# Four image layers on one core: another order of full layers and causal pieces, merged score matmuls, and work moved from VectorE to ScalarE and GpSimd

## The chip, the core and the metric

The kernel runs on one core of one Trainium2 chip. The metric is the device time of one execution in microseconds (us), lower is better; the time before is the median of three runs. The engines are TensorE (PE; its weight loads are PEld), VectorE (DVE), ScalarE (ACT), GpSimd (POOL) and SyncE (SP), which issues the DMAs.

## The reference, cut to what matters

x is float32, (4, 256, 32, 32): four batches of 256 channels and 1024 pixels. Four layers follow each other, each batch for itself:

- **L0**: attention over the 1024 pixels with 32-wide queries and keys, `gamma * out + x`.
- **L1** and **L3**: group normalisation (32 groups), attention over the 1024 pixels with 256-wide queries, keys and values, an output projection, and the residual.
- **L2**: the pixels as 1024 tokens of 256 values. Token normalisation, causal attention with 8 heads of 32 that share one key and value head, an output projection added to the tokens, token normalisation with gain and shift, then a feed-forward part: normalisation, a 256x256 product, normalisation, gelu, a 256x256 product, and the residual.

```python
x = _L0_conv_ref(x, ...)
x = _L1_conv_ref(x, ...)
x = _L2_conv_ref(x, ...)
x = _L3_conv_ref(x, ...)
```

## The kernel before, in words

There are two chains of work, woven on every engine. The **full chain** (F) holds the twelve full layers L0, L1 and L3 of the four batches in the order `FULL` (line 35). The **causal chain** (C) holds a few weight products and then L2 of batches 0 to 3, in the order that `causal_schedule` (line 159) gives. Each chain is a generator that yields after every step. `ORDER` (line 43) has a string for each engine, one letter a step: on PE, `F` or a digit takes the next full step, `C` or a letter a to h the next causal one, and the digit or the letter a to h also names the PSUM bank at which the step opens its unit. Every engine works through its string in order, and an instruction that waits holds back all that stand behind it. So L0 of a batch needs x in SBUF, L1 needs L0, batch b of C needs L1.b, and L3.b needs batch b of C.

Products that need more than one rounding of float32 are made of a high and a low part: ACT writes the high part (a cast to float32r), DVE the low part (the value less the high part), PE does three passes, high with high, high with low, low with high (`product`, line 675).

A **full layer** on PE has projections (q, k, v), for each of eight tiles of 128 queries the scores (`full_scores`, line 705, two steps), transposes of the probabilities (`full_turn`, line 718), and for each quarter of 256 queries the values (`full_values`, line 727, four steps of eight instructions, line 732). DVE takes the maximum of each row, ACT the exponent, DVE scales, ACT evicts the transposes, DVE adds the residual. L1 and L3 begin with group statistics (`group_means`, `group_normed`), which need all of the batch's tiles. L3 of batches 0 to 2 works in the tensor z, L3 of batch 3 in x[0] (`home`, line 369).

**L2 of a batch** has eight blocks of one head group (4 heads) and 256 queries. `causal_max` (line 933) makes the scores of a tile of 128 queries against up to 512 keys, head by head, and behind each head's score matmul, where the keys reach the diagonal, a matmul of the bf16 mask (lines 946 and 948). DVE reduces them to maxima (line 1565). `causal_exponents` (line 951) makes the scores again, transposed, one matmul for each of four heads, over 256 queries (128 in the last piece of a block), and ACT takes the exponent (line 1205); POOL masks diagonal pieces (line 658). `causal_values` (line 963) is the product with the values and with ones. `normalise` (line 1579) inverts the sums, scales, and makes the high and low part of the heads (lines 1586 to 1593), all on DVE.

The **feed-forward part** follows a quarter of the tokens behind: wo, ln2b, f1b, ta, w1, f2b, tg, w2 (line 91). A token normalisation is `norm_start` on DVE (statistics, mean and variance, variance plus eps at line 1463), the power -0.5 on POOL (`root`, line 637, with line 643), and `norm_end` on DVE: `(x - mean) * rstd` at line 1479, or with gain and shift at line 1482. PE transposes the result (line 881); ta and tg are the transposes in front of the two feed-forward products. After tg ACT takes the gelu (line 1184) and DVE writes its high and low part (lines 1543, 1544). w2 first multiplies the tokens by the identity (line 916), then adds the product; ACT evicts it to the home of L3. The first w2 of batches 1 and 2 waits for the earlier batch's store: `pe.wait_ge(y_out, 16 * NB * b)`.

## Time and profile before

| | us |
|---|---|
| median of 3 runs | 1485.58 |
| lowest and highest | 1484.95, 1488.01 |
| the profiled execution, its own time | 1486.03 |
| its span, first to last instruction | 1484.2 |
| granted TensorE clock over the span, mean | 0.958 |

A row of a group names line, engine, operation, output and inputs, shapes and count, then busy time, mean time of one in ns, and the idle time in front. A timeline row has start and busy time; matmuls overlap, so what a matmul costs in a stream is the distance from its start to the next start. The clock is a share of 2.4 GHz: 1.00 is 2.4 GHz throughout, 0.5 would be 1.2 GHz throughout. The page's section 6 gives the load of one batch of x (1024 KB) as landing 6.5 us after its issue.

### The profile page before, as it was taken

Reading aid. Unit: us, or ns where it says so; the run is one execution under the profiler, and the core shown is the slowest. Engines: PE = TensorE matmul, PEld = TensorE weight load, DVE = VectorE, ACT = ScalarE, POOL = GpSimd, SP = SyncE. Lnnn points to the kernel's source line nnn. Section 1 sums busy time; section 2 is a strip of 40 time slices with the busy share of each in tenths; the row PEclk is TensorE's granted clock in tenths of the full one; section 3 lists DMA queues with packets and bytes.
Section 4 is the critical chain, followed back from the end, with each engine's and each line's share of the span. In section 5 each row is a group of like instructions: output and inputs, shape, how many; then the busy total and the mean of one; then the engine's idle time right before and its main releaser. Section 6 shows DMA issues by size and latency. Waiting matters only on the chain.

```text
span 1484.2 us, 22513 instructions
## 1 busy us (share of the span) xinstructions
PE 1338.0 (90%) x9152; PEld 1067.9 (72%) x9152; DVE 870.6 (59%) x1854; ACT 595.3 (40%) x973; POOL 92.5 (6%) x134
## 2 busy tenths in 40 slices
PE   5889989999999899989997899988999899998498
PEld 5768766777778777767776777776678777765486
DVE  3634466776458567557456657727656667675442
ACT  3523334344355343435334534423544443444142
POOL 0000000000000000000000000000010001001000
PEclk9999989999999899999998999997999999999699
DMA  5000010000000200010000010010000100100000
GB/s 176 1 1 0 29 43 23 1 23 2 1 1 2 70 11 14 22 29 1 2 1 0 6 38 23 2 49 3 1 2 1 43 2 23 37 16 1 0 1 29
DMA packets 20613, 27.09 MB, mean 18 GB/s; under 512 B 3488, under 2 KB 14240, under 8 KB 20512
## 3 DMA queue, kind: packets, MB, share of 16 engines
q1 hardware_dynamic: 20512, 25.66, 6.2%
q8 instruction: 74, 1.21, 0.3%
q14 instruction: 27, 0.22, 0.1%
HBM read 8.61 MB, written 4.19 MB: 9 GB/s over the span
## 4 chain that ended last, share of the span: by engine, by line
PE 79%; DVE 9%; ACT 6%; issue 2%; DMA 1%; SPq 1%; POOL 0%; ACTq 0%; DVEq 0%
PE ring L679 27%; PE ring L732 22%; PE ring L978 9%; PE ring L946 5%; PE ring L959 5%; PE ring L723 4%; ACT probs L1036 2%; PE ring L760 1%; PE ring L881 1%; ACT probsT L1049 1%; ACT cprobs L1205 1%; PE ring L948 1%; PE ring L916 1%; DVE part_max L1565 1%; SPq L595 1%
## 5 line engine op out<-in xcount | busy, mean ns | idle before, releaser
L732 PE MATMUL ring<-probsT,vt 128*128 128x256 f32 x1536 | 358.5, 387 | 16.7 <-ACT probsT L1049 16.4
L732 PEld LDWEIGHTS ring<-probsT,vt 128*128 128x128 f32 x1536 | 288.6, 193 | 67.4 <-ACT probsT L1049 20.6
L1205 ACT ACTIVATE cprobs<-ring 128x1024 f32<-128x1024 f32 (+1 forms) x160 | 150.4, 942 | 247.6 <-PE ring L959 246.9
L1036 ACT ACTIVATE probs<-ring,neg_max 128x1024 f32<-128x1024 f32 x96 | 107.1, 1116 | 185.4 <-DVE neg_max L1282 87.7
L1565 DVE TENSOR_REDUCE part_max<-ring 128x2 f32<-128x1024 f32 (+2 forms) x112 | 127.2, 1143 | 47.6 <-PE ring L946 34.2
L946 PE MATMUL ring<-ks,qs 96*128 96x512 f32 (+3 forms) x384 | 129.8, 421 | 16.4 <-ACT cprobs L1205 3.7
L1049 ACT COPY probsT<-ring 128x512 f32<-128x512 f32 x192 | 102.3, 592 | 48.2 <-PE ring L723 48.2
L959 PE MATMUL ring<-qs,ks 98*128 98x256 f32 (+1 forms) x640 | 114.5, 302 | 5.8 <-ACT probs L1036 1.4
L1281 DVE TENSOR_REDUCE shift_max<-ring 128x1 f32<-128x1024 f32 x64 | 78.3, 1224 | 70.3 <-PE ring L679 68.4
L723 PE MATMUL ring<-consts,probs 128*128 128x128 f32 x768 | 106.7, 279 | 13.1 <-ACT probs L1036 7.3
L959 PEld LDWEIGHTS ring<-qs,ks 98*128 98x128 f32 x640 | 91.4, 192 | 27.4 <-issue 15.6
L723 PEld LDWEIGHTS ring<-consts,probs 128*128 128x128 f32 x768 | 88.0, 143 | 32.1 <-ACT probs L1036 8.5
L679 PE MATMUL ring<-h_hi,q_hi 128*128 128x512 f32 x256 | 106.5, 416 | 3.6 <-ACT probs L1036 3.2
L946 PEld LDWEIGHTS ring<-ks,qs 96*128 96x128 f32 x384 | 77.4, 211 | 34.6 <-issue 10.4
L679 PE MATMUL ring<-h_hi,q_lo 128*128 128x512 f32 x256 | 100.5, 392 | 0.0
L679 PE MATMUL ring<-h_lo,q_hi 128*128 128x512 f32 x256 | 100.2, 392 | 0.0
L978 PE MATMUL ring<-cprobs,v 128*32 128x256 f32 (+1 forms) x1280 | 96.9, 375 | 0.0
L978 PE MATMUL ring<-cprobs,ones 128*32 128x256 f32 (+1 forms) x1280 | 92.9, 362 | 0.0
L643 POOL TENSOR_TENSOR rstd<-var_eps,half_neg 128x2 f32<-128x2 f32 (+1 forms) x56 | 44.8, 801 | 538.2 <-DVE var_eps L1463 538.2
L658 POOL TENSOR_SCALAR_AFFINE_SELECT cprobs<-cprobs 128x512 f32<-128x512 f32 x64 | 41.9, 657 | 540.6 <-ACT cprobs L1205 540.5
L1293 DVE TENSOR_SCALAR probs<-probs,row_inv 128x1024 f32<-128x1024 f32 x96 | 72.4, 754 | 3.4
L679 PEld LDWEIGHTS ring<-h_hi,q_hi 128*128 128x128 f32 x256 | 48.2, 188 | 19.9 <-issue 7.9
(215 smaller groups left out, 2212.1 us busy)
## 6 DMA issues: line engine op xcount, KB each, us to landing
x<-x_dram SPq DMA_DIRECT2D x4, 1024.0 KB, 6.5
qs<-q_hi SPq DMA_DIRECT2D x32, 128.0 KB, 2.3
qs<-q_hi SPq DMA_DIRECT2D x64, 64.0 KB, 2.0
out_dram<-z SPq DMA_DIRECT2D x6, 512.0 KB, 2.8
qs<-q_lo SPq DMA_DIRECT2D x16, 128.0 KB, 2.3
qs<-max_rows SPq DMA_DIRECT2D x128, 2.0 KB
qs<-q_lo SPq DMA_DIRECT2D x32, 64.0 KB, 2.0
out_dram<-x SPq DMA_DIRECT2D x2, 512.0 KB, 2.8
```

The source lines that it names most:

```text
L679: ins = mm(out, w, m, start=first and n == 0, stop=last and n == len(every) - 1)
L723: last = nc.tensor.transpose(o[:, j, :], probs[:, ti % 2, (TPH * hf + j) * P:(TPH * hf + j + 1) * P], ident)
L732: last = mm(o[:, ct * QUARTER:(ct + 1) * QUARTER], vt[:, j, ct * P:(ct + 1) * P], probsT[:, qi % (NQ - 1), j, :], start=j == 0, stop=j == ...
L946: last = mm(o, stack(k, a, 3 * DH, at, at + P), ks[0:3 * DH, lo:hi], start=True, stop=not diag)
L959: last = mm(heads(name)[:, a, 0:n], ks[0:3 * DH + 2, jt * P:(jt + 1) * P], stack(k, a, 3 * DH + 2, QUARTER - n, QUARTER), start=True, stop ...
L978: last = mm(acc[DH * a:DH * (a + 1), (half + 1) * QUARTER - n:(half + 1) * QUARTER], w, causal_probs(step, n)[:, a, :], start=jt == 0 and ...
L1036: A(probs[:, ti % 2, :], flat(full_name(l, b, ("s", ti))), ACT.Exp, bias=neg_max[:, ti:ti + 1], accum_out=row_sum[:, ti:ti + 1]).then_inc( ...
L1049: nc.scalar.copy(probsT[:, ti // 2 % (NQ - 1), js, (ti % 2) * P:(ti % 2 + 1) * P], slot(name)[:, 0, :].rearrange("p (s n) -> p s n", n=P)) ...
L1205: A(causal_probs(step, n), heads(name)[:, :, 0:n], ACT.Exp).then_inc(read_done["c", "act"], 1)
L1281: full_then(v.tensor_reduce(shift_max[:, ti:ti + 1], flat(name), AX_X, ALU.max, negate=True))
L1293: v.tensor_scalar(probs[:, ti % 2, :], probs[:, ti % 2, :], row_inv[:, ti:ti + 1], None, ALU.mult).then_inc(probs_scaled["dve"], 1)
L1565: v.tensor_reduce(cols if ti < TPH else parts[:, ch, :], src[:, :, 0:n], AX_X, ALU.max, negate=True).then_inc(read_done["c", "dve"], 1)
```

## The change

- `FULL`: L1.3 now comes before L3.1. `home` gives every batch's L3 the place z, x[1], x[0], z, and L0 and L1 of batch 3 the place z. The PE wait for the store in front of w2 goes; SP loads batch 2 behind the transposes of batch 0 as before, batch 3 behind the two stores of L3.0. The group statistics of L3 get two buffers.
- `ORDER`: new strings for every engine. In the old one the last 58 causal steps on PE stand alone behind the last step of L3.2; in the new one L3.1 and L3.2 stand among the steps of batch 3 (PE steps 987 to 1256, counted from 0), and L3.2's last four steps come behind batch 3's last. L3.3 follows in both, alone, with the same letters.
- Score matmuls: an exponent piece over 256 queries is two matmuls of 512 columns (two heads each), one over 128 queries a single one of 512 columns. In a piece of maxima the masks follow all of the score matmuls.
- The three normalisations without gain move `norm_end` to ACT, as `scale * x + bias` with scale rstd and bias -mean * rstd. DVE adds a negated mean, POOL the product (`offset`). The high cast of the heads and of the gelu moves to ACT, and the division of a block becomes four pieces, with up to two taken at a place.

```diff
@@ -32,7 +32,7 @@
 
 
 
-FULL = [("L0", 0), ("L1", 0), ("L0", 1), ("L1", 1), ("L0", 2), ("L3", 0), ("L1", 2), ("L0", 3), ("L3", 1), ("L1", 3),
+FULL = [("L0", 0), ("L1", 0), ("L0", 1), ("L1", 1), ("L0", 2), ("L3", 0), ("L1", 2), ("L0", 3), ("L1", 3), ("L3", 1),
         ("L3", 2), ("L3", 3)]
 
 
@@ -42,42 +42,42 @@
 
 ORDER = {
     "PE": (
...
-        "70bcbeagbd4gF12dCg0eFbhcCegbCFFhceaCh2FeaeC67cga4Fh3ghcC60ebCFdgbfCdFFbgfda6F4dcCCaCdC0bc674FFacCgaFcCa5g5cg"
-        "ha5cFaCFgdaCgCFcaCegcaCecahecaCcegaCCbCdCfCgaCcCegahCcCheCaChCCChfCgahabC72F406F2F4062F450F672F450FFF6F541F3"
...
+        "6hFFhF707FgfFFCbd0g1F3fh02Fe5F024hagc4Fh601dF73eeagcda5Fhcace7aca10fFFhCdbF4agbCF73acgC0Fef734afChFafFFfCdha"
+        "5FhehdC4201f4cCfFabdCfFF0bfhda22FgfCCdCaCbfFF0ceCaceCcaeghcaeC2gaeCbCFecCagecCa2gea1g3bfFCb5Fd1hgCCd1Cf3C1hC"
+        "Fd45gC1gFCd5g01FdhC0d5C7bFcCFeCFaC1CFCh0d64F210ChFFF3F5672ba7FFgfF46C0FFF72F406F2F4062F450F672F450FFF6F541F3"
...
@@ -90,7 +90,7 @@
 
 FEED_FORWARD = ("wo", "ln2b", "f1b", "ta", "w1", "f2b", "tg", "w2")
 LAG = 2
-NORM_PIECES = 3
+NORM_PIECES = 4
 LN_SLOTS = 4
 
 
@@ -175,7 +175,7 @@
         for i, e in enumerate(base):
             events.append(e)
             events += [f for at, f in fill if at == i]
-            if divide:
+            for _ in range(min(len(divide), 1 + len(divide) // NORM_PIECES)):
                 events.append(divide.pop(0))
             if is_final(e):
                 divide += norm(e[1])
...
@@ -366,8 +367,11 @@
         h_full = shared("h_full", [P, CT, N], r_p)
         probsT = shared("probsT", [P, NQ - 1, NT, QUARTER], r_t)
 
+        def gn_stats(l, b):
+            return all_stats[l][:, b % 2 if l == "L3" else 0, :, :, :]
+
         def home(l, b):
-            return x[b % 2] if l != "L3" else x[0] if b == B - 1 else z
+            return (z, x[1], x[0], z)[b] if l == "L3" else (x[0], x[1], x[0], z)[b]
 
         xs = shared("xs", [P, NT, C], r_xs)
         an = shared("an", [P, NT, C], r_an)
...
@@ -569,11 +576,14 @@
             sp.dma_start(home("L0", 1)[:, :, :], x_dram[1]).then_inc(x_in[1], 16)
 
             def full_chain():
-                for b in range(2, B):
-                    wait_filled(sp, f"C{b - 2}.xt1")
-                    sp.dma_start(home("L0", b)[:, :, :], x_dram[b]).then_inc(x_in[b % 2], 16)
-                    yield
-                for b in range(B):
+                wait_filled(sp, "C0.xt1")
+                sp.dma_start(home("L0", 2)[:, :, :], x_dram[2]).then_inc(x_in[0], 16)
+                yield
+                yield from stores(0)
+                sp.wait_ge(y_out, 16 * NB)
+                sp.dma_start(home("L0", 3)[:, :, :], x_dram[3]).then_inc(x_in[1], 16)
+                yield
+                for b in range(1, B):
                     yield from stores(b)
 
             def stores(b):
@@ -642,6 +652,10 @@
                 pool.wait_ge(var_ready, b * NORMS + n + 1)
                 pool.tensor_tensor(rstd[:, s, 0:w], var_eps[:, s, 0:w], half_neg[:, 0:w],
                                    ALU.pow).then_inc(rstd_ready, 1)
+                if name in by_act:
+                    pool.wait_ge(rstd_ready, b * NORMS + n + 1)
+                    pool.tensor_tensor(offset[:, s, 0:w], neg_mean[:, s, 0:w], rstd[:, s, 0:w],
+                                       ALU.mult).then_inc(offset_ready, 1)
 
             def causal_chain():
                 for b in range(B):
@@ -908,8 +922,6 @@
                     wait_read(pe, f"C{b}.ta{hf}")
                     token_project(name, hn[hf % 2], ffw1, 0, n)
                 elif kind == "w2":
-                    if 0 < b < B - 1 and hf == 0:
-                        pe.wait_ge(y_out, 16 * NB * b)
                     o = open_unit(name)[:, 0, :].rearrange("p (c n) -> p c n", c=CT)
                     for co in range(CT):
                         for i in range(n):
@@ -940,12 +952,16 @@
                 open_unit(name)
                 diag = hi == (ti + 1) * P
                 at = (ti - qi * TPQ) * P
-                for i in range(4) if two == 2 else range(2):
-                    o = heads(name)[:, i, 0:hi - lo] if two == 2 else slot(name)[:, i, 0:hi - lo]
+                own = 4 // width[name] if two == 2 else 1
+                outs = [(heads(name) if two == 2 else slot(name))[:, i, 0:hi - lo] for i in range(4 if two == 2 else 2)]
+                for i, o in enumerate(outs):
                     a = i if two == 2 else 2 * two + i
-                    last = mm(o, stack(k, a, 3 * DH, at, at + P), ks[0:3 * DH, lo:hi], start=True, stop=not diag)
-                    if diag:
-                        last = mm(o[:, hi - lo - P:hi - lo], mask[:, 0, :], mask[:, 1, :], start=False, stop=True)
+                    last = mm(o, stack(k, a, 3 * DH, at, at + P), ks[0:3 * DH, lo:hi], start=i % own == 0,
+                              stop=not diag and i % own == own - 1)
+                if diag:
+                    for i, o in enumerate(outs):
+                        last = mm(o[:, hi - lo - P:hi - lo], mask[:, 0, :], mask[:, 1, :], start=False,
+                                  stop=i % own == own - 1)
                 last.then_inc(filled["c"], 1)
 
             def causal_exponents(b, e):
@@ -955,9 +971,10 @@
                     pe.wait_ge(shift_in[k % 2], 64 * (K // 2 * b + k // 2 + 1))
                 name = causal_name(b, e)
                 open_unit(name)
-                for a in range(4):
-                    last = mm(heads(name)[:, a, 0:n], ks[0:3 * DH + 2, jt * P:(jt + 1) * P],
-                              stack(k, a, 3 * DH + 2, QUARTER - n, QUARTER), start=True, stop=True)
+                own = 4 // width[name]
+                for a in range(0, 4, own):
+                    last = mm(heads(name)[:, a:a + own, 0:n], ks[0:3 * DH + 2, jt * P:(jt + 1) * P],
+                              stack(k, slice(a, a + own), 3 * DH + 2, QUARTER - n, QUARTER), start=True, stop=True)
                 last.then_inc(filled["c"], 1)
 
             def causal_values(b, e):
@@ -1154,10 +1171,23 @@
                 A(wq[l][0][:, :, :], qk_product(l), ACT.Identity, scale=C ** -0.5).then_inc(prep_hi, 1)
                 yield
 
+            def normed(b, name, src, t0, n):
+
+                s = (b * NORMS + norm_no[name]) % LN_SLOTS
+                act.wait_ge(offset_ready, b * len(by_act) + by_act.index(name) + 1)
+                for i in range(n):
+                    last = A(an[:, t0 + i, :], src[:, t0 + i, :], ACT.Identity, scale=rstd[:, s, i:i + 1],
+                             bias=offset[:, s, i:i + 1])
+                last.then_inc(ln_ready, 1)
+
             def stage(b, e):
                 kind, hf = e
                 name = causal_name(b, e)
                 sl = token_half(hf)
+                if e == ("xn", 0) or e == ("kv", 0):
+                    i = 0 if kind == "xn" else 1
+                    normed(b, f"ln1.{i}", xs, i * TPH, TPH)
+                    yield
                 if kind == "xt":
                     wait_filled(act, name)
                     nc.scalar.copy(xs[:, hf * TPH:(hf + 1) * TPH, :].rearrange("p t c -> p (t c)"),
...
@@ -1213,8 +1250,16 @@
                             nc.scalar.copy(sums[:, k % 2, :], acc[:, QUARTER:])
                             nc.scalar.copy(nums[:, hg, token_quarter(qi)],
                                            acc[:, 0:QUARTER]).then_inc(read_done["c", "act"], 1)
-                        elif len(e) == 2 and e[0] not in NO_UNIT + ("vt", "wo", "w1"):
-                            stage(b, e)
+                        elif e[0] == "norm":
+                            if e[2] != 2:
+                                continue
+                            hg, qi = BLOCKS[e[1]]
+                            to = token_quarter(qi)
+                            act.wait_ge(heads_scaled, b * K + e[1] + 1)
+                            nc.scalar.copy(heads_out[0][:, hg, to], nums[:, hg, to]).then_inc(heads_hi, 1)
+                        elif len(e) == 2 and e[0] not in ("vt", "wo", "w1", "ln2b"):
+                            yield from stage(b, e)
+                            continue
                         else:
                             continue
                         yield
@@ -1307,7 +1352,7 @@
                 if l == "L0":
                     wait_read(dve, name)
                     for ct in range(CT):
-                        ins = v.bn_stats(gn_stats["L1"][:, ct, qi, :], dst[:, ct, sl])
+                        ins = v.bn_stats(gn_stats("L1", b)[:, ct, qi, :], dst[:, ct, sl])
                     if qi == NQ - 1:
                         full_then(ins)
                     yield
...
@@ -1470,21 +1516,14 @@
                     causal_then(ins)
                     yield
 
-            def norm_end(b, name, src, t0, n, dst, shift=None):
+            def norm_end(b, name, src, t0, n, dst, shift):
 
                 s = (b * NORMS + norm_no[name]) % LN_SLOTS
                 dve.wait_ge(rstd_ready, b * NORMS + norm_no[name] + 1)
                 for i in range(n):
-                    if shift is None:
-                        ins = v.tensor_scalar(dst[:, t0 + i, :], src[:, t0 + i, :], ln_mv[:, s, i, 0:1],
-                                              rstd[:, s, i:i + 1], ALU.subtract, ALU.mult)
-                    else:
-                        ins = v.scalar_tensor_tensor(out=dst[:, t0 + i, :], in0=src[:, t0 + i, :],
-                                                     scalar=rstd[:, s, i:i + 1], in1=shift, op0=ALU.mult, op1=ALU.add)
-                if shift is None:
-                    ins.then_inc(ln_ready, 1)
-                else:
-                    causal_then(ins)
+                    ins = v.scalar_tensor_tensor(out=dst[:, t0 + i, :], in0=src[:, t0 + i, :],
+                                                 scalar=rstd[:, s, i:i + 1], in1=shift, op0=ALU.mult, op1=ALU.add)
+                causal_then(ins)
                 yield
 
             def stage(b, e):
...
@@ -1533,20 +1568,16 @@
                     wait_read(dve, name)
                     yield from norm_start(b, f"f2.{hf}", an, t0, n)
                     return
-                elif kind == "f2b":
-                    yield from norm_end(b, f"f2.{hf}", an, t0, n, an)
-                    return
                 elif kind == "tg":
                     first, second = act2[hf % 2]
                     src = gelu[hf % 2][:, :, :]
-                    wait_read(dve, name)
-                    causal_then(v.tensor_copy(first[:, :, :], src))
+                    dve.wait_ge(act2_hi, b * NQ + hf + 1)
                     v.tensor_tensor(second[:, :, :], src, f32(first[:, :, :]),
                                     ALU.subtract).then_inc(act2_ready, 1)
                 elif kind == "w2":
                     wait_read(dve, name)
                     for c in range(CT):
-                        ins = v.bn_stats(gn_stats["L3"][:, c, hf, :], home("L3", b)[:, c, token_quarter(hf)])
+                        ins = v.bn_stats(gn_stats("L3", b)[:, c, hf, :], home("L3", b)[:, c, token_quarter(hf)])
                     if hf == NQ - 1:
                         ins.then_inc(z_ready, 1)
                 yield
@@ -1586,10 +1617,12 @@
                     ins = v.reciprocal(den[:, piece * P:(piece + 1) * P], den[:, piece * P:(piece + 1) * P])
                     if piece:
                         causal_then(ins)
+                elif piece == 2:
+                    to = token_quarter(qi)
+                    v.tensor_tensor(nums[:, hg, to], nums[:, hg, to], den, ALU.mult).then_inc(heads_scaled, 1)
                 else:
                     to = token_quarter(qi)
-                    causal_then(v.tensor_tensor(nums[:, hg, to], nums[:, hg, to], den, ALU.mult))
-                    causal_then(v.tensor_copy(heads_out[0][:, hg, to], nums[:, hg, to]))
+                    dve.wait_ge(heads_hi, b * K + k + 1)
                     v.tensor_tensor(heads_out[1][:, hg, to], nums[:, hg, to], f32(heads_out[0][:, hg, to]),
                                     ALU.subtract).then_inc(out_ready, 1)
 
...
```

## Rows read from the trace of the kernel before

**Rows 1.** Page, section 1: busy us, share of the span, instructions of each engine.
```profile
PE 1338.0 (90%) x9152; PEld 1067.9 (72%) x9152; DVE 870.6 (59%) x1854; ACT 595.3 (40%) x973; POOL 92.5 (6%) x134
```

**Rows 2.** Page, section 4: the chain that ended last, shares of the span.
```profile
PE 79%; DVE 9%; ACT 6%; issue 2%; DMA 1%; SPq 1%; POOL 0%; ACTq 0%; DVEq 0%
```

**Rows 3.** Windows of four stretches: PE, PEld, DVE, ACT, POOL busy, clock, DMA, GB/s.
```profile
0.00:172.00 172.00, 142.81 (x759) 123.77 (x760) 74.12 (x160) 60.69 (x113) 2.08 (x8) 0.97 0.12 39
172.00:1322.00 1150.00, 1067.84 (x7529) 842.53 (x7526) 723.39 (x1531) 479.59 (x772) 82.56 (x115) 0.97 0.06 16
1322.00:1398.00 76.00, 54.25 (x497) 38.78 (x496) 41.41 (x100) 27.31 (x38) 7.19 (x10) 0.82 0.02 8
1398.00:1484.20 86.20, 73.10 (x374) 62.78 (x374) 31.64 (x64) 27.67 (x51) 0.70 (x1) 0.95 0.03 13
```

**Rows 4.** Waits of PE from 1322 to 1406: us in total, times, longest.
```profile
PE ring L881 <- DVE an L1479: 12.2, 3, 6.9
```

**Rows 5.** Timeline of PE, three places: start us, busy us, engine, line, operation.
```profile
251.00 0.66 PE L959 MATMUL ring<-qs,ks 98*128 98x128 f32 x4
251.59 0.64 PE L978 MATMUL ring<-cprobs,v 128*32 128x256 f32 x8
...
252.59 1.97 PE L723 MATMUL ring<-consts,probs 128*128 128x128 f32 x16
...
268.33 0.36 PE L946 MATMUL ring<-ks,qs 96*128 96x256 f32 x1
268.53 0.23 PE L948 MATMUL ring<-mask 128*128 128x128 bf16 x1
268.57 0.36 PE L946 MATMUL ring<-ks,qs 96*128 96x256 f32 x1
...
364.72 0.39 PE L679 MATMUL ring<-h_hi,q_lo 128*128 128x512 f32 x1
364.94 0.64 PE L959 MATMUL ring<-qs,ks 98*128 98x256 f32 x4
365.42 0.34 PE L946 MATMUL ring<-ks,qs 96*128 96x384 f32 x1
```

**Rows 6.** Groups by line and shape: busy us, mean ns; idle before.
```profile
L959 PE MATMUL ring<-qs,ks 98*128 98x256 f32 x512 | 93.7, 306 | 5.7 <-ACT probs L1036 1.4 <-DMA qs<-max_rows 1.4 <-DVE part_max L1565 1.1
...
L948 PE MATMUL ring<-mask 128*128 128x128 bf16 x256 | 60.9, 244 | 0.0
...
L643 POOL TENSOR_TENSOR rstd<-var_eps,half_neg 128x2 f32<-128x2 f32 x48 | 36.4, 757 | 406.3 <-DVE var_eps L1463 406.3
...
L1479 DVE TENSOR_SCALAR an<-xs,ln_mv,rstd 128x256 f32<-128x256 f32 x64 | 22.8, 408 | 7.0 <-POOL rstd L643 6.9
...
L1184 ACT ACTIVATE gelu<-ring,vecs 128x256 f32<-128x256 f32 x32 | 16.3, 561 | 26.0 <-PE ring L881 26.0
...
L1592 DVE CAST heads_out_hi<-nums 128x256 fp32r<-128x256 f32 x32 | 10.0, 313 | 1.1
```

**Rows 7.** Timeline at the first w2 of batch 1, PE.
```profile
643.02 2.00 PE L916 MATMUL ring<-consts,xs 128*128 128x128 f32 x8 [1.65 <-DMA out_dram<-z]
...
645.03 0.41 PE L679 MATMUL ring<-act_lo,ffw_hi 128*128 128x256 f32 x1
...
645.24 0.41 PE L679 MATMUL ring<-act_hi,ffw_lo 128*128 128x256 f32 x1
```

**Rows 8.** Timeline at the start of L3.3.
```profile
1399.56 0.84 ACT L1190 ACTIVATE x<-ring,vecs 128x256 f32<-128x256 f32 x2 [2.96 <-PE ring L679]
...
1402.13 0.39 PE L750 MATMUL ring<-gn_in,consts 128*128 128x4 f32 x2 [2.60 <-DVE gn_in L1326]
...
1406.12 0.77 PE L760 MATMUL ring<-h_hi,L_wqk_hi 128*128 128x512 f32 x1 [3.60 <-issue]
```

**Rows 9.** Timeline, POOL and DVE at 1320 us.
```profile
1320.02 1.27 POOL L658 TENSOR_SCALAR_AFFINE_SELECT cprobs<-cprobs 128x512 f32<-128x512 f32 x2
1320.09 1.35 DVE L1479 TENSOR_SCALAR an<-an,ln_mv,rstd 128x256 f32<-128x256 f32 x2 [0.81 <-POOL rstd L643]
```

More of the change, by code:

```diff
@@ new lines @@
+        "aCFgC506bCFf32a5CgFCcFeaFgC2aCFf7601cC5gCFaCFCFCdc104FFFCh5F2F04F6F2a4F1a62F704F16cd7FCeaFF2F640F57c6FahFF4F"
+        "3h2670bedgFbFhF12egace5gFaFFecgafc4gabdCef0F2hefCahcC35FabdfCabdfCdab5hehdCFacC0fec5eC0cf2ahFe60e2gbCF01C4Fc"
+        "C6a1C0cFeFbdFC5bdFdC0b7d1faFh03e6bFdCFafFbC3gFC5a26aC3ea2FdfFCaFdfh01ce6FaCFceFabCC0cCeCgCa1F35dC0F5F2aC4ag2"
+        "eh0CFc7C52eF7a5C0cFC75eC2CFChFgF0F75Ce2F670FFF4F3c106h5FFFed21Cg0FFFe2Fg0F4ch0F4F2g0F745F230F7e4fc3acFFhFeac"
+        "geea2F674F01cgceag1ceFfFFhCca3F5670cbdCfha2CFFbdfaCdF4f4a4FFaCcfgFabacCdfCb7fdgCbdfabd5hbCCcCeChbF315FdbCdfb"
@@ L308, in build @@
     norm_no = {name: i for i, name in enumerate(norms)}
+    by_act = [name for name in norms if not name.startswith("ln2")]
     ready = [("xt", 0), ("xt", 1)] + [e for e in schedule if e[0] in ("f1b", "f2b")]
@@ L432, in build @@
         var_eps, rstd = sb("var_eps", [P, LN_SLOTS, 4]), sb("rstd", [P, LN_SLOTS, 4])
+        neg_mean, offset = sb("neg_mean", [P, LN_SLOTS, 4]), sb("offset", [P, LN_SLOTS, 4])
         ln_stats, ln_mv = sb("ln_stats", [P, LN_SLOTS, TPH, 6]), sb("ln_mv", [P, LN_SLOTS, TPH, 2])
@@ L1186, in stage @@
                     last.then_inc(read_done["c", "act"], 1)
+                    wait_read(act, name)
+                    nc.scalar.copy(act2[hf % 2][0][:, :, :], gelu[hf % 2][:, :, :]).then_inc(act2_hi, 1)
                 elif kind == "w2":
@@ L1192, in stage @@
                     last.then_inc(read_done["c", "act"], 1)
+                elif kind == "f1b":
+                    normed(b, f"f1.{hf}", xs, hf * TPQ, TPQ)
+                elif kind == "f2b":
+                    normed(b, f"f2.{hf}", an, hf * TPQ, TPQ)
+                yield
             def causal_chain():
@@ L1462, in norm_start @@
                 causal_then(ins)
+                if name in by_act:
+                    v.tensor_scalar(neg_mean[:, s, 0:n], ln_mv[:, s, 0:n, 0], -1.0, None, ALU.mult)
                 v.tensor_scalar(var_eps[:, s, 0:n], ln_mv[:, s, 0:n, 1], EPS_LN, None, ALU.add).then_inc(var_ready, 1)
@@ L1500, in stage @@
                     yield from norm_start(b, f"ln1.{hf}", xs, hf * TPH, TPH)
-                    yield from norm_end(b, f"ln1.{hf}", xs, hf * TPH, TPH, an)
                     return
@@ L1523, in stage @@
                     return
-                elif kind == "f1b":
-                    yield from norm_end(b, f"f1.{hf}", xs, t0, n, an)
-                    return
                 elif kind == "ta":
@@ L1610, in causal_chain @@
                             normalise(b, e)
-                        elif len(e) == 2 and e[0] != "shift":
+                        elif len(e) == 2 and e[0] not in ("shift", "f1b", "f2b"):
                             yield from stage(b, e)
```

62 lines of the change are left out of this document (28 added, 34 removed).

## The prediction

> **What bounds the kernel now.** The page's first section comes first: TensorE (PE) is busy 90% of the span, VectorE (DVE) 59%, ScalarE (ACT) 40%, GpSimd (POOL) 6% [rows 1]. The chain of waits says that this is no accident: 79% of it is PE, 9% DVE, 6% ACT [rows 2]. So time goes away only where PE's own work gets smaller or where PE stands still or runs slow. The windows show where that is [rows 3]. There are four stretches: the first layers nearly alone (172 us), nine full layers among the causal pieces (1150 us, PE busy 93%, granted clock 0.97), the end of the last causal batch alone (76 us, PE busy 71%, clock 0.82), and L3.3 alone (86 us). In the third PE idles 21.8 us, 12.2 of them in 3 waits for normalised tokens [rows 4]: a serial chain over DVE, POOL and ACT with nothing beside it.
>
> **Merged score matmuls, on PE's path.** An exponent piece over 256 queries is four matmuls of 256 columns, 0.48 us from its start to the next piece's; a 512-column matmul takes 0.23 us from start to start [rows 5]. Two of those are 0.46, so 128 pieces (512 matmuls, [rows 6]) save 0.02 each, 2.6 us. A piece over 128 queries takes 0.59 us to the next start [rows 5]; one 512-column matmul with the same 0.1 us of change-over and set-up takes about 0.37. 32 of them save 0.22 each, 7.0 us. A mask behind its own score matmul makes 0.24 us for the pair, against 0.12 for a 256-column matmul alone [rows 5], so 0.12 a mask. There are 256 masks [rows 6], in 32 pieces of four and 64 of two. Put at the end of their piece, the first keeps its 0.12 and no row shows the others: at best 0.04 (mask to next start, [rows 5]), at worst its 0.12 again. I take 0.06, nearer the mask's own row. That is 32 x 0.18 + 64 x 0.06 = 9.6 us, bounds 0 and 12.8. Together 19 us, bounds 9 and 25 (a third of the exponents' gain added as error of reading). The Trainium skill, "TensorE: Matmul & The Clock Gate", section on the back-to-back issue gap, gives 131 ns as the sustained gap at 512 columns; an estimate by it makes the 256-query merge worth 128 x (0.48 - 0.26) = 28 us, and the sum 25 us lower. The trace disagrees: 0.23 us in a full stream.
>
> **The order of the full layers.** Before, the last 58 causal steps stand behind the last full step of L3.2: the 76 us of rows 3. Counted with the same spacings they hold 43 us of PE work: 18 pieces of values 16.7 (one of 256 queries takes 1.0 us, from 251.59 to 252.59, [rows 5]; 3 are of 128 queries at 0.58), 16 exponent pieces 7.6, scores with masks 4.5, 72 projection matmuls at 0.12, 44 transposes at 0.115. After, L3.1 and L3.2 both run beside batch 3, and L3.2 ends four steps behind the last causal step. In the overlapped stretch the same count gives 987 us of work in 1150, 0.86; idle and clock there would allow 0.90 [rows 3]. 43 / 0.86 is 50 us, so 26 us go. Bounds: 0 (the loss only moves elsewhere, since nine layers are spread over the same four batches) and 33.
> What covers the chain then can be counted too: three steps of values (1.73 us each), the last scores and four transpose steps stand between the last output projection and its normalised tokens, 5.2 + 2.8 + 1.8 = 9.8 us (twelve score matmuls, four steps of four transposes) against PE's longest wait of 6.9 us there [rows 4].
>
> **Homes of the batches.** L3.1 and L3.2 keep their tiles in x, so the first residual matmul of w2 no longer waits for L3's store. PE waited 1.65 us for it at 643 [rows 7], as long again for L3.1's at 1002, and behind it the matmuls start 0.21 us apart instead of 0.12 [rows 7]: the clock is at its lower level, 1.2 GHz, for about 3 us. 5 us go. Against it x of batch 3 is loaded only behind L3.0's store, on SP's queue. Its landing (6.5 us in the page's section 6) has 99 PE steps between L3.0's last and L0.3's first, and what is queued behind that wait on SP are batch 2's stacks, also far off. Nothing.
>
> **The head of L3.3.** Before, PE stood 2.6 us for the group statistics and 3.6 us for h [rows 8], then ran at 1.2 GHz. The four steps of L3.2's last values, 6.9 us, now lie over the 6.5 us from the last w2 (its eviction begins at 1399.56) to PE's restart at 1406.12 [rows 8]. 7 us go, bounds 0 and 8.
>
> **Normalisation, high casts, offset.** Off DVE go 96 tensor-scalars of 0.41 to 0.46 us (64 and 32), 32 casts of 0.31 and 16 of 0.42: 53 us [rows 6]. 40 negated means come, each like the small scalar operation beside them (0.17), 7 us. DVE ends 46 us lighter. ACT gets 96 activations: the gelu one of the same size with two pointer operands takes 0.56 us [rows 6], a plain copy 0.39; with pointers it is nearer gelu's, less overlap, 0.5. With the casts (32 x 0.39, 16 x 0.6) that is 70 us on an engine 40% busy, which becomes 46%. POOL gets 40 products at 0.70 to 0.76 [rows 6], 30 us at 6% busy. None is PE work; the cover is PE's queue of other pieces in the overlap. The chain itself gets longer: 0.7 for the offset, 0.1 for its wait, about 0.2 for ACT's slower pair, and whatever ACT has in hand. Where the cover fails, at ta and tg, PE waited 12.2 us in the tail [rows 4] and 1 us elsewhere; I charge 3 us net, with -15 (the lighter DVE pays) and +25 as ends.
> One rule speaks against the offset on GpSimd. The trace shows it: beside two affine selects the pair at line 1479 took 1.35 us [rows 9], against 0.82 for two by their mean [rows 6]. The Trainium skill, "SBUF — State Buffer", section on SBUF's two separate sides, calls the pair of ports that VectorE and GpSimd share an exclusive lock. If each of 40 products caught such a pair, 40 x 0.53 = 21 of DVE's 46 us would be given back; that takes from the larger-gain rival, not from the sum, which credits DVE's relief nowhere.
>
> **Sum.** 1484.2 - 19 - 26 - 5 - 7 + 3 = 1430.2 us of span. The profiled run lies 1.8 us above its span (1486.0 against 1484.2), and the median of the runs 0.5 below that: 1432 us.
>
> **Rivals.**
> A, slower: in-order queues. ACT's normalisation waits for the offset at the head of its queue with the exponents behind it; DVE's low parts wait for ACT's casts with the row maxima behind them. 88 such handoffs (40, 32, 16). Fully exposed they cost 1.8, 0.7 and 0.7 us, 106 us: 1432 + 103 = 1535. The gain of 52 us is gone when about 0.6 us a handoff shows on PE, half of it; that would be 1484 and beyond, and I put this case at 1500. For: PE waited for exactly these producers in the tail. Against: in the 1150 us of overlap PE is 93% busy and DVE 63%, so most of it has cover, and the new order was laid for other due times than the old.
> B: the rearrangement gives nothing, since the solo loss spreads over the batches; only the merge and half of the rest remain: 1467 us. For: the full layers are the filler, and their sum is unchanged.
> C: DVE's relief counts. Outside the named places PE still idles some 85 us (146 idle in all, less 22 in the tail, 29 at the start, 10 at L3.3 and the stores). A quarter of that goes: 1412 us. For: DVE is 9% of the chain.
> D: nothing changes, the handoffs eat what the merge and the order bring: 1484 us.
>
> **How the numbers follow.** Forecast 0.56 (1418 to 1448 by its bounds), B 0.17, C 0.16, A 0.08, D 0.03. The range of 8 in 10 leaves out A, D and the outer parts of B and C: 1406 to 1467. A change within 0.2% (3 us) can't be told from none here. Faster 0.90, same 0.03, slower 0.07.
>
> **What would show it.** PE with 8800 matmuls (256 fewer at 256 queries, 96 at 128), and mask matmuls under 0.1 us apart. PE busy above 90% up to the last causal step, and a granted clock over 0.9 there. No PE wait on a store. DVE near 825 us, ACT near 665, POOL near 120. PE's restart in L3.3 behind values without a 3 us gap. Wrong would be: PE waits on ACT's normalised tokens or on DVE behind ACT's casts of more than 40 us in sum (A), or PE idle in the overlap up from 82 to over 110 us (B).

## The result

| | before | after |
|---|---|---|
| median, us | 1485.26 (4 runs) | 1444.44 (4 runs) |
| lowest and highest | 1484.59, 1488.01 | 1440.94, 1447.75 |
| span of the profiled execution | 1484.2 | 1439.0 |
| granted TensorE clock, mean | 0.958 | 0.969 |

The ratio is 0.9721, with a 95% interval of 0.9695 to 0.9748: 41 us less, where the prediction said 53 (1432, range 1406 to 1467). Direction and range hold. Of the five terms of the sum, the order and the head of L3.3 came out far too large, the split has the wrong sign, and the homes gave two thirds of what was forecast, as the experiments show.

The page of the kernel after, sections 1 and 4, answers to [rows 1, 2]:

```profile
PE 1312.9 (91%) x8800; PEld 1019.1 (71%) x8800; DVE 818.3 (57%) x1750; ACT 662.8 (46%) x1119; POOL 101.3 (7%) x174
...
PE 78%; DVE 10%; ACT 9%; issue 2%; DMA 1%; SPq 0%; POOL 0%; ACTq 0%; DVEq 0%
```

8800 matmuls, DVE 52 us lighter, ACT 67 us heavier. The chain is still PE's; ACT's share of it went from 6% to 9%.

Windows of the kernel after, columns as in [rows 3]; the second line is everything from the end of the first layers to the group statistics of L3.3:

```profile
0.00:170.00 170.00, 140.51 (x746) 121.78 (x746) 71.11 (x155) 60.39 (x112) 2.28 (x9) 0.97 0.12 39
170.00:1355.00 1185.00, 1099.35 (x7692) 834.92 (x7692) 716.65 (x1538) 575.59 (x958) 98.34 (x164) 0.97 0.06 16
1355.00:1439.00 84.00, 73.06 (x362) 62.37 (x362) 30.56 (x59) 26.83 (x49) 0.70 (x1) 0.94 0.05 19
```

The slow stretch at the end of the last batch (76 us at clock 0.82, [rows 3]) is gone. Its 76 us and the 1150 in front of it, 1226 in all, became 1185, with PE idle for 86 us instead of 104. (Taken up to the same place in the work, the end of PE's last matmul before L3.3's statistics at 1399.5 and at 1353.7, it is 1227.5 and 1183.7 us, with 104 and 84 us of idle time.)

Groups by shape, kernel after, answering to [rows 6]:

```profile
L976 PE MATMUL ring<-qs,ks 98*128 98x512 f32 x288 | 108.9, 451 | 13.4 <-ACT cprobs L1242 5.4 <-DVE part_max L1596 5.0 <-ACT probs L1053 1.6
...
L963 PE MATMUL ring<-mask 128*128 128x128 bf16 x256 | 32.8, 233 | 0.0
...
L1179 ACT ACTIVATE an<-xs,offset,rstd 128x256 f32<-128x256 f32 x64 | 34.1, 595 | 33.5 <-POOL offset L657 33.5
...
L1259 ACT CAST heads_out_hi<-nums 128x256 fp32r<-128x256 f32 x32 | 13.0, 408 | 62.5 <-DVE nums L1622 62.4
...
L657 POOL TENSOR_TENSOR offset<-neg_mean,rstd 128x2 f32<-128x2 f32 x32 | 6.3, 196 | 2.5
```

The moved operations stand in front of waits: ACT is idle 62.4 us before casts of heads and 42.9 us before normalisations (33.5 and 9.4, two shapes). The question is how much of that PE feels.

The head of L3.3, timeline of the kernel after (start us, busy us; idle before in brackets), against [rows 8]:

```profile
1353.77 0.88 DVE L1348 SCALAR_TENSOR_TENSOR x<-ring,L_bvo,x 128x256 f32<-128x256 f32 x2 [5.29 <-PE ring L746]
1354.57 0.26 DVE L1365 BATCH_NORM_AGGREGATE gn_mv<-gn_stats 128x2 f32<-128x24 f32 x1
...
1355.47 0.39 PE L764 MATMUL ring<-gn_in,consts 128*128 128x4 f32 x2 [1.74 <-DVE gn_in L1370]
...
1359.46 0.76 PE L774 MATMUL ring<-h_hi,L_wqk_hi 128*128 128x512 f32 x1 [3.61 <-issue]
```

The cover was expected from L3.2's last four value steps. It fails: DVE takes the residual behind those steps first and starts the statistics only then, so both gaps are still there.

### The profile page after: what moved, and what is told of

Its sections match the earlier page's. It is cut to its first block, busy times and chain, and to the rows that moved or that the text cites. A ratio compares the mean times of both kernels' runs of the same rounds, so it can differ in the third digit from the quotient of the medians.

```text
span 1439.0 us, 21864 instructions
## 1 busy us (share of the span) xinstructions
PE 1312.9 (91%) x8800; PEld 1019.1 (71%) x8800; DVE 818.3 (57%) x1750; ACT 662.8 (46%) x1119; POOL 101.3 (7%) x174
## 4 chain that ended last, share of the span: by engine, by line
PE 78%; DVE 10%; ACT 9%; issue 2%; DMA 1%; SPq 0%; POOL 0%; ACTq 0%; DVEq 0%
PE ring L693 26%; PE ring L746 23%; PE ring L995 9%; PE ring L976 4%; PE ring L959 4%; PE ring L737 3%; DVE part_max L1596 2%; ACT probs L1053 2%; PE ring L895 1%; PE ring L774 1%; ACT probsT L1066 1%; ACT cprobs L1242 1%; PE ring L928 1%; PE ring L963 1%; DVE ln_stats L1500 1%
## 5 line engine op out<-in xcount | busy, mean ns | idle before, releaser
L959 PE MATMUL ring<-ks,qs 96*128 96x512 f32 (+3 forms) x384 | 113.4, 395 | 18.0 <-DVE part_max L1596 5.3
L976 PE MATMUL ring<-qs,ks 98*128 98x512 f32 x288 | 108.9, 451 | 13.4 <-ACT cprobs L1242 5.4
L959 PEld LDWEIGHTS ring<-ks,qs 96*128 96x128 f32 x384 | 64.9, 204 | 46.5 <-issue 17.0
L976 PEld LDWEIGHTS ring<-qs,ks 98*128 98x128 f32 x288 | 49.2, 196 | 35.4 <-issue 12.6
```

Of the source, the lines that this page charges most:

```text
L959: last = mm(o, stack(k, a, 3 * DH, at, at + P), ks[0:3 * DH, lo:hi], start=i % own == 0, stop=not diag and i % own == own - 1)
L976: last = mm(heads(name)[:, a:a + own, 0:n], ks[0:3 * DH + 2, jt * P:(jt + 1) * P], stack(k, slice(a, a + own), 3 * DH + 2, QUARTER - n, QU ...
```

## The experiments

The edits are shown abridged, with comments added. In the ledger below, all from the one profiled execution of a kernel, "idle" is the span less PE's busy time, and "low clock" is (1 - mean clock) x span, what the time at 1.2 GHz costs while PE works; "rest" is the remainder. The clock has three digits, so a term is good to about 1 us by reading. Two things make it rougher. Executions of one kernel differ in clock: those of e1 had 0.953 to 0.959, those of e6 0.961 to 0.968, which is 9 and 10 us of low clock. And where PE is idle at the low clock the time is in both terms: rest spans 1268 to 1285 us over the eight kernels with the same 9152 matmuls, lowest where PE idles most. So rest is read here only between two kernels that differ in the matmuls alone, and a few us of it mean nothing. "On ACT", "on DVE" are the sums of PE's idle time by the engine that ended it, over all lines of PE's waits. The ratio is to runs of before on the same chip (medians 1485.0 to 1486.4), and "gain" is (ratio - 1) x 1485.6.

| kernel | median | ratio, 95% interval | gain | idle | low clock | rest | on ACT | on DVE |
|---|---|---|---|---|---|---|---|---|
| before | 1485.3 | | | 146 | 62 | 1276 | 52.6 | 66.5 |
| homes only (e5) | 1482.4 | 0.9978, 0.9969-0.9988 | -3.3 | 143 | 62 | 1275 | | |
| merging only (e1) | 1479.1 | 0.9948, 0.9934-0.9962 | -7.7 | 147 | 69 | 1261 | | |
| homes and order (e3) | 1474.6 | 0.9930, 0.9915-0.9945 | -10.4 | 132 | 59 | 1282 | 40.2 | 76.0 |
| + merging (e6) | 1458.7 | 0.9821, 0.9796-0.9845 | -26.6 | 136 | 51 | 1270 | 39.6 | 79.6 |
| + casts on ACT (e8) | 1463.3 | 0.9844, 0.9825-0.9863 | -23.2 | 140 | 51 | 1270 | 45.1 | 76.9 |
| e6 + normalisation on ACT (e9) | 1449.9 | 0.9756, 0.9736-0.9776 | -36.2 | 124 | 57 | 1269 | 47.9 | 61.7 |
| after (all) | 1444.4 | 0.9721, 0.9695-0.9748 | -41.4 | 126 | 45 | 1268 | 53.9 | 57.9 |
| after, unmerged (e2) | 1462.2 | 0.9849, 0.9834-0.9865 | -22.4 | 122 | 53 | 1285 | | |
| after + head (e7) | 1438.5 | 0.9675, 0.9655-0.9696 | -48.3 | 122 | 43 | 1272 | 54.4 | 56.7 |
| old order, whole split (e4) | 1578.5 | 1.0620, 1.0604-1.0636 | +92.1 | 206 | 104 | 1268 | 120.2 | 60.0 |
| old order, normalisation on ACT (e11) | 1539.2 | 1.0374, 1.0343-1.0406 | +55.6 | 179 | 83 | 1272 | 92.4 | 61.6 |
| old order, casts on ACT (e12) | 1536.7 | 1.0343, 1.0327-1.0359 | +51.0 | 179 | 86 | 1270 | 80.9 | 71.3 |
| e12, casts behind the exponent (e14) | 1524.7 | 1.0276, 1.0262-1.0290 | +41.0 | 164 | 87 | 1270 | 69.8 | 67.7 |

"The split" is the move of normalisation, casts and offset. Where it is undone or done alone, the letters of the moved steps are taken out of or put into ORDER's strings for ACT and DVE (a new step on ACT right ahead of that chain's next one), and all else of the strings stays. So these runs ask what an operation costs in an order that was laid for its absence or presence, not what a fresh order could make of it.

**Merging alone (e1)**, in the kernel before:

```diff
-                for a in range(4):
-                    last = mm(heads(name)[:, a, 0:n], ...)
+                own = 4 // width[name]
+                for a in range(0, 4, own):
+                    last = mm(heads(name)[:, a:a + own, 0:n], ...)
```

and the same lines of `causal_max` as in the change.

> The kernel before with nothing but the merged exponent matmuls and the masks behind all score matmuls of a piece. Prediction as put: 19 us less, 1466. Theory after reading the trace of after (like pieces between like neighbours: 0.16 us saved on an exponent piece of 128 queries, 0.005 on one of 256, 0.22, 0.05, 0.07 and 0.00 on the four kinds of masked pieces): 12 us less, 1473. Rival: the saved time is waited away again in an order laid for the old costs, 1483 to 1486.

7.7 us, between the expectations. By the ledger it is not the 15 that rest fell by because low clock is 7 higher; by the middle clock of e1's six executions (0.9545) it is 5 higher. The one of them with a clock of 0.959 took 1474.1 us, 12 less than before, the other five (0.953 to 0.955) 1478.5 to 1480.4.

**Homes alone (e5)**: `home`, the loads on SP, the statistics' buffers and the wait in front of w2 as in the change, all else as before.

```diff
-                    if 0 < b < B - 1 and hf == 0:
-                        pe.wait_ge(y_out, 16 * NB * b)
```

> The kernel before with the new homes of the batches, no wait for the store in front of w2, and batch 3 loaded behind the stores of L3.0; same order of layers, no merge, no move between engines. Prediction: 5 us less, 1480. Rival: PE waits the same time for the next thing that is late there (the transposes of batch 3 or the group statistics), 1484 to 1486.

3.3 us for a term of 5; its interval, 1.8 to 4.6, ends just short of it. PE's waits on the store, 3.3 us in all before, are gone, and so is the low clock behind the first of them: the matmuls that started 0.21 us apart [rows 7] now start 0.12 apart, as the timeline of e5 shows:

```profile
641.65 0.28 PE L685 MATMUL ring<-act_hi,ffw_hi 128*128 128x256 f32 x1
641.77 0.28 PE L685 MATMUL ring<-act_lo,ffw_hi 128*128 128x256 f32 x1
```

From 643 to 646 us the clock is 1.00 and was 0.52. But the mean over the span stayed at 0.958, so the low clock came back elsewhere and only the idle time was gained.

**Homes and order (e3)**: the changed kernel with score matmuls separate, and normalisation and casts on DVE.

```diff
-FULL = [..., ("L0", 3), ("L3", 1), ("L1", 3),
+FULL = [..., ("L0", 3), ("L1", 3), ("L3", 1),
```

> New order of layers and pieces with the new homes, but matmuls unmerged and normalisation and casts on DVE as before (the moved DVE steps are put close behind the step before them). Prediction's terms: 5 + 26 + 7 us less, 1447; without the head of L3.3, which the trace of after shows unchanged (PE idle 1.7 and 3.6 us there), 1454. Rival B: the layers are only filler moved about, nothing beyond the homes, 1478 or more. Rival: this order needs the lighter DVE, so it comes out at 1465 to 1485 without the move.

10.4 us together (8.2 to 12.6), so 7 for the order, against 26. The slow stretch is gone here too, but most of what it cost is now in the overlap. Window of e3 over the same steps, up to L3.3:

```profile
172.00:1390.00 1218.00, 1123.93 (x8038) 878.34 (x8038) 761.38 (x1639) 509.81 (x814) 90.75 (x125) 0.96 0.06 16
```

PE is busy 1124 us of 1218; before it was 1122 of 1226 [rows 3]. The idle time fell by 10 us (12 when both end with PE's last matmul before the statistics), and 3 of these are the homes'. The low clock over the whole span fell by 3. PE's waits on ACT fell by 12 us and those on DVE rose by 10: more of PE's idle time was now ended by DVE.

**The whole split in the old order (e4)**:

```diff
-                    for i in range(n):
-                        v.tensor_scalar(an[:, t0 + i, :], ..., mean, rstd)   # DVE
+                normed(b, name, src, t0, n)                                   # ACT
+                    nc.scalar.copy(heads_out[0][:, hg, to], nums[:, hg, to])  # ACT
```

> Normalisation, high casts and offset moved as in the change, in the old order of layers with the old homes and unmerged matmuls. Prediction: 3 us more, 1488, with -15 and +25 as ends. Rival A, in-order queues: over 0.6 us at each of 88 handoffs, 1530 or more. Rival C, the lighter DVE pays: 1465 to 1475.

Rival A in full: 92 us for the 88 handoffs, 1.05 us each. Idle time rose by 60 us and low clock by 42 (rest is 8 lower, the double count). All of the added idle time is on ACT: 120 us in place of 53. Loads of ACT's function tables are not the reason: there are 31 in this kernel and 31 before. Of the runs, all but e1 and e5 carry the four-piece division of the change (both reciprocals at one place of DVE's queue); no run takes it out by itself, so the order's 7 us and the costs in the old order have it in them.

**No split in the new order (e6)** and **no merging in the changed kernel (e2)**: the same diffs backwards.

> The changed kernel with token normalisation and the casts of heads and gelu back on VectorE: order, homes and merged matmuls stay. Additive theory: order and homes gave 11.8 us alone and merging 7.2 us alone, so 1486 - 19 = 1467, and the split is worth the rest to 1444, 23 us. Rival 'the split is worth its forecast of nothing': 1444 to 1450, order and merging reinforce each other. Rival 'the split still costs a little here': under 1443.

> The changed kernel with every score matmul of two sequences' pieces issued separately, as before. By the spacing of like neighbours in the two traces merging saves 12 us of TensorE: 1456 if all of it is on the path. By the first run of merging alone (7.2 us of 12) 1451 to 1452. Rival 'merging is hidden by the waits on other engines': 1444 to 1446.

From e3 to e6 merging gives 16 us, from e2 to after 19. Rest falls by 12 and 17 us, near the 15 of e1; but here low clock falls by 8 as well (by 6 and 8 with the middle clock of each kernel's executions), where it rose by 7 in e1. The split, 92 us dear in the old order, gives 15 us in the new (e6 to after). PE's waits on DVE fall by 22 us, those on ACT rise by 14.

**Only the normalisation back on DVE (e8), only the casts back (e9)**:

```diff
-                normed(b, f"ln1.{i}", xs, i * TPH, TPH)                       # ACT, e8
+                yield from norm_end(b, f"ln1.{hf}", xs, hf * TPH, TPH, an)    # DVE, e8
...
-                nc.scalar.copy(act2[hf % 2][0][:, :, :], gelu[hf % 2][:, :, :])   # ACT, e9
+                causal_then(v.tensor_copy(first[:, :, :], src))                   # DVE, e9
```

> The changed kernel with the token normalisation alone back on VectorE (its mean subtracted and multiplied in one instruction, no offset on GpSimd); the casts stay on ScalarE. If the split pays by taking work from VectorE, half of it goes back (96 instructions, some 26 us of VectorE more than the casts' share): 1452 to 1458. If the chain of three engines (VectorE, GpSimd, ScalarE) ahead of the projections costs as much as it saves, as the two waits of 6.1 and 2.4 us in the changed kernel's trace hint, 1438 to 1444.

> The changed kernel with the high casts of heads (32) and gelu (16) back on VectorE; the token normalisation stays on ScalarE. Two runs so far disagree with 'less on VectorE is always faster': with the normalisation on VectorE, moving the casts to ScalarE made 1458.7 into 1463.3. If the casts' move costs those 4.6 us here too (ScalarE waits 62 us in all for the scaled heads, with exponents behind), 1438 to 1441. Rival 'the casts' 23 us of VectorE matter once its queue is the short one': 1448 to 1456.

The normalisation carries the split's gain: 18 us with the casts on ACT (e8 to after), 10 without (e6 to e9). The casts give 5 us with the normalisation on ACT and cost 3 without it; in both pairs the intervals overlap, so their sign is open.

**The old order with one half of the split (e11, e12)**: edits as in e4, the other half left on DVE.

> The kernel before with only the token normalisation on ScalarE and its offset on GpSimd, in the old order; casts on VectorE, score matmuls unmerged. The whole split cost 92 us in the old order. If the chain VectorE, GpSimd, ScalarE ahead of the projections carries that (TensorE waits 24 us there in the whole split's trace, 18 of ScalarE's waits are on the offset), 1545 or more. If the casts carry it, 1495 or less. If each delays the other's engine and neither alone is bad, 1500 to 1530 in both.

> The kernel before with only the high casts of heads and gelu on ScalarE, in the old order; normalisation on VectorE, score matmuls unmerged. If the casts carry the 92 us (ScalarE stands 98 us in all at the scaled heads, up to 6.2 us at a time, and the exponents behind it are what TensorE waits for), 1545 or more. If the normalisation's chain carries it, 1495 or less.

56 and 51 us. Neither expectation of a single culprit holds, nor the third one, 1500 to 1530 in both: each half alone costs more than half of the 92. The two together have 15 us more than the whole split. That would fit a cost of the division in four pieces, common to all three, but it was not tried by itself, and the halves may as well overlap in what they delay. How a cast costs so much is to be seen in e12's timeline:

```profile
374.29 1.22 DVE L1308 TENSOR_REDUCE shift_max<-ring 128x1 f32<-128x1024 f32 x1 [0.50 <-PE ring L686]
...
375.68 0.94 DVE L1611 RECIPROCAL sums<-sums 128x128 f32<-128x128 f32 x1
376.66 1.22 DVE L1590 TENSOR_REDUCE part_max<-ring 128x2 f32<-128x1024 f32 x1
377.80 0.41 DVE L1616 TENSOR_TENSOR nums<-nums,sums 128x256 f32<-128x256 f32 x1
378.25 0.40 ACT L1241 CAST heads_out_hi<-nums 128x256 fp32r<-128x256 f32 x1 [6.13 <-DVE nums L1616]
378.56 1.02 ACT L1224 ACTIVATE cprobs<-ring 128x1024 f32<-128x1024 f32 x1
...
379.63 0.55 PE L730 MATMUL ring<-consts,probs 128*128 128x128 f32 x3 [4.00 <-ACT cprobs L1224]
```

The cast stands at the head of ACT's queue for 6.1 us, from 372.1 on. In that time DVE does the block's two reciprocals (the first, not shown, at 372.84) and two maxima before it scales the heads. The scores of the next exponent were done at 375.6 (four matmuls from 374.91 on, not shown); it waits behind a 0.4 us cast until 378.56, and PE stands for 4.0 us until it is through.

**The casts behind the exponent (e14)**: e12, and the 28 casts that have an exponent behind them are issued after it.

```diff
                             A(causal_probs(step, n), heads(name)[:, :, 0:n], ACT.Exp)...
+                            cast_held()
...
-                            act.wait_ge(heads_scaled, b * K + e[1] + 1)
-                            nc.scalar.copy(heads_out[0][:, hg, to], nums[:, hg, to]).then_inc(heads_hi, 1)
+                            held.append((b, e[1]))
```

> The previous run (old order, casts on ScalarE, 1537) with one thing moved: 28 of the 32 casts of the scaled heads are issued on ScalarE after the exponent that stood behind them, instead of before it; the other 4 (the last block of each pair) stay. If those 51 us come from ScalarE standing at the cast with a ready exponent behind it, most of them go: 1490 to 1510. Rival 'the cost is the path itself' (VectorE stands at the low part until the cast is done, with the maxima behind it, and now waits for one exponent of about 0.9 us more): 1537 to 1560. Rival 'the cost is the clock or the gelu casts': about 1537.

A miss between the expectations. ACT's wait lines, first e12, then e14:

```profile
ACT heads_out_hi L1241 <- DVE nums L1616: 100.9, 31, 6.2
```

```profile
ACT heads_out_hi L1224 <- DVE nums L1626: 36.9, 18, 4.5
```

64 us of ACT's standing went and 10 us of time with it (1.0343 to 1.0276), PE's waits on ACT fell by 11. So the queue head is a cause, worth a fifth of the 51 us, net of what the later casts may cost. The low clock did not move (86 and 87, against 62 before), and where the other 41 us come from is open. Two things that e14 leaves as they are were not tried by themselves: the four pieces of the division, and the gelu casts, for which DVE's low part waits 29.5 us in e12 and 29.4 in e14.

**The head of L3.3 closed (e7)**: the changed kernel, with the statistics ahead of the last residual on DVE and the group sums between the last value steps on PE.

```diff
+                    if n == len(FULL) - 2:
+                        early = group_normed(*FULL[-1], n + 1, normed + 1)
+                        for _ in range(3):
+                            next(early)
+                            yield
                     yield from residual(l, b, NQ - 1)
```

> The changed kernel with the group statistics of full layer 3 of the last pair taken by VectorE before the last residual of full layer 2, and TensorE's group sums placed between that layer's last value steps. If the two gaps of 1.7 and 3.6 us at the head of that layer are there because VectorE does the residual first, they close: 1438 to 1440, with no gap over 1 us in TensorE between the two layers. Rival 'the wait only moves, since the residual is now late for the layer's own start': 1443 to 1446.

Timeline of e7 at the same place:

```profile
1353.10 0.26 DVE L1377 BATCH_NORM_AGGREGATE gn_mv<-gn_stats 128x2 f32<-128x24 f32 x1
...
1354.69 0.28 PE L767 MATMUL ring<-gn_in,consts 128*128 128x4 f32 x2
1354.83 3.70 PE L749 MATMUL ring<-probsT,vt 128*128 128x256 f32 x16
...
1358.57 0.47 PE L777 MATMUL ring<-h_hi,L_wqk_hi 128*128 128x512 f32 x1
1358.64 0.88 DVE L1360 SCALAR_TENSOR_TENSOR x<-ring,L_bvo,x 128x256 f32<-128x256 f32 x2 [0.68 <-PE ring L749]
1358.88 0.39 PE L777 MATMUL ring<-h_hi,L_wqk_lo 128*128 128x512 f32 x1
1359.11 0.40 PE L777 MATMUL ring<-h_hi,L_wqk_hi 128*128 128x512 f32 x1
```

The same matmuls in the changed kernel:

```profile
1360.45 0.63 PE L774 MATMUL ring<-h_hi,L_wqk_hi 128*128 128x512 f32 x1
1360.87 0.63 PE L774 MATMUL ring<-h_hi,L_wqk_lo 128*128 128x512 f32 x1
```

No bracket on PE's lines: the gaps of 1.74 and 3.61 us are gone, and the residual moved behind L3.3's h at no cost. The clock held as well: the projections start 0.31 and then 0.23 us apart, at a clock of 1.00, where in the changed kernel they start 0.42 apart behind the gaps, at 1.2 GHz. 1438.5 us beats both kernels, with 0.9675 (0.9655 to 0.9696) against 0.9721 (0.9695 to 0.9748). That is 7 us by the ratios where 4 to 6 were expected; the intervals just touch, and the two profiled executions lie only 2.5 us apart in span (1439.0 and 1436.5). So the closed gaps are shown by the trace, and their worth lies somewhere between 2.5 and 7 us.

## Why the prediction was right, and where it was not

**Merged matmuls, 19 forecast.** PE's work fell by 12 to 17 us (rest, three pairs). The estimate for a mask held. Timeline of PE after, a piece of four masks, a 128-query piece, a 256-query one, each with the next start:

```profile
269.61 0.40 PE L963 MATMUL ring<-mask 128*128 128x128 bf16 x4
269.84 0.61 PE L895 MATMUL ring<-consts,an 128*128 128x128 f32 x4
...
275.22 0.50 PE L976 MATMUL ring<-qs,ks 98*128 98x512 f32 x1
275.66 0.64 PE L995 MATMUL ring<-cprobs,v 128*32 128x256 f32 x8
...
301.89 0.63 PE L976 MATMUL ring<-qs,ks 98*128 98x512 f32 x2
302.36 1.09 PE L780 MATMUL ring<-h_lo,L_wqk_hi 128*128 128x512 f32 x4
```

0.23 / 4 = 0.06 a mask, as taken. A merged 128-query piece takes 0.44 us and not 0.37, so it saves 0.15 (32 x 0.15 = 5 us for 7), and one of 256 queries 0.47 for 0.48, about 1 us for 2.6. So two merged matmuls take what four small ones took, as the spacing of 0.23 us in the stream had said. The Trainium skill, "TensorE: Matmul & The Clock Gate", section on the back-to-back issue gap, gives 131 ns at 512 columns, from which the prediction estimated 28 us for this merge; the trace does not agree. What the step lacked was the clock: it priced work at full clock, and what merging brings in time was 7.7 us in the old order and 16 to 19 in the new, where the low-clock term rose by 7 and fell by 8.

**The order, 26 forecast, 7 measured alone.** This is the step that failed: "43 / 0.86 is 50 us, so 26 us go". The stretch vanished, but the step assumed that the overlap would take the moved work at its old share of 0.86. The forecast's lower bound named the reason, the loss only moves elsewhere, and rival B was built on it. It is rival B for the order by itself. The price that the rival had, 1467, is the merge alone; with the half of the other terms that its text grants (4.5 us) it would be 1462. In the whole change the order is worth more than by itself, since with it merging pays twice as much and the split pays where it cost.

**Homes, 5 forecast, 3.3 measured.** The 3.3 us of waits went. The rest of the term was the stretch at 1.2 GHz behind them; it went at its place, but the mean clock stayed at 0.958, so it brought nothing.

**The head of L3.3, 7 forecast, 0.9 us of gap gone** (2.60 and 3.60 us before, 1.74 and 3.61 after). "The four steps of L3.2's last values now lie over the 6.5 us": they do on PE, but the step never asked in which order DVE works. The residual of those same values stands ahead of the statistics in DVE's queue. e7 turns the two round, and both gaps close.

**Normalisation, casts and offset, +3 forecast, -15 measured in this order.** The sum had "DVE's relief nowhere"; it is rival C at a smaller size, and its end of the bounds. The relief is seen as 22 us less of PE's waits on DVE. In the old order the same edit is rival A at 1.05 us a handoff, beyond its point of break-even of 0.6. So both rivals were true mechanisms, and which one held went with the order of the queues; what in the old order makes the cost is shown only in part (e14). The offset was priced too dear: a product of two columns takes 0.20 us on POOL, not the 0.70 of the power beside it; with 40 of them POOL rose by 9 us and not by 30. For DVE's operations slowed beside GpSimd's the prediction allowed 21 us. It compared its 1.35 us pair, which normalises `an` in place, with the mean of the other shape (0.408 us); the mean of its own is 0.457, so the bound is 40 x 0.44 = 18. No run here isolates it.

**Sum.** Forecast -19 - 26 - 5 - 7 + 3 = -54 of span; the ladder e5, e3, e6, after measures -3 (homes), -7 (order), -16 (merging), -15 (split), 41 together. Four terms fell short by 31 us together, and the fifth gave 18 more than forecast. So the range held in part by luck: a failed cover and an overrated order stood against a gain on DVE that was booked as a small loss.

Of the signs named: 8800 matmuls, mask matmuls 0.06 apart, a clock of 0.97 in the overlap, PE busy 93% there, DVE 818 and ACT 663 came as said; POOL was 101 and not 120; PE waited in all 54 us on ACT, against 53 before, so A did not come, and only one wait on normalised tokens is large, 6.1 us where batch 3 begins; PE's restart in L3.3 kept its gap. The sign for B, over 110 us of idle time in the overlap, did not show either (86, and 94 in e3), though the order by itself did what B says: the sign was set too high to see it, since PE's idle time before, with the slow stretch, was 104 us.

## What to carry to other kernels

An operation that moves to another engine's in-order queue is priced by its place there, not by its duration: a 0.4 us cast held ACT for 6 us and PE for 4, and the same edit cost 92 us in one order and gave 15 in another. Look, for each moved instruction, at what is queued behind it and when its input is ready, and lay the order again with the move. Try the parts in the order in which they will live: here the parts in the old order (3 and 8 us of gain, 92 of loss) and the new order by itself (7 of gain) do not add up to the 41 us that they gave together. When work is put over a serial chain as cover, follow the chain on every engine: the cover's own epilogue may stand ahead of it.

## What the runs showed that was not expected

The same saving of PE's work came out as different times, and the granted clock is where they part. Merging took 15 us from PE's work in the old order and 12 to 17 in the new, but the low-clock term went from 62 to 69 us in the one (clock 0.958 to 0.953) and from 59 to 51 and 53 to 45 in the other. The split in the old order raised it from 62 to 104 us (0.958 to 0.934), 42 of its 92 us. In the four old-order kernels with parts of the split, 18 to 60 us of added idle time came with 21 to 42 us of added low clock, so PE's idle time alone did not tell what a wait cost. The clock differs between executions of one kernel too: those of e6 took 1452.3 us at 0.968 and 1465.1 at 0.961. What decides it is not shown by these runs.
